# Where a routed expert layer hands over from its early tiles to its late ones: order of VectorE's steps, TensorE's filler products, SyncE's row numbers and GpSimd's scatters

## What is computed

```python
xn = layernorm(x)
# feed-forward part of layer 0 (after its own attention, which gives x_mid)
h2     = rmsnorm(x_mid, ln2_w)                       # (2048, 128)
top1   = argmax(h2 @ Wr + br)                        # one of E = 8 experts for each token
u      = h2 @ W1[top1] + b1[top1]                    # 512 columns
y      = (u[:256] * sigmoid(u[256:])) @ W2[top1] + b2[top1]
x      = x + attention(xn) + x_mid + y
# layer 1: layernorm(x), a state-space block and a four-matrix gated network, added to x
```

## Time and profile before

| | |
|---|---|
| median of 3 runs | 592.8 us (592.77, 592.80, 595.66) |
| profiled execution, its own time | 592.8 us |
| its span, first to last instruction | 590.9 us |
| TensorE busy | 557.3 us, 94% |
| ScalarE busy | 471.3 us, 80% |
| VectorE busy | 396.6 us, 67% |
| GpSimd busy | 121.2 us, 21% |
| mean granted clock of TensorE | 0.997 |

### The profile page before, as it was taken

The page is one execution under the profiler, slowest core; times in us unless marked ns, Lnnn a source line. Parts: engine busy times, 40 slices in busy tenths (PEclk is TensorE's granted clock), DMA queues, the critical chain, the costliest instruction groups (busy, mean ns, idle before and its releaser), DMA issues.

```text
span 590.9 us, 11199 instructions
## 1 busy us (share of the span) xinstructions
PE 557.3 (94%) x3932; PEld 330.4 (56%) x3932; DVE 396.6 (67%) x1056; ACT 471.3 (80%) x670; POOL 121.2 (21%) x161
## 2 busy tenths in 40 slices
PE   6799999999999999999998899798799999999998
PEld 3344333443443434334435587386678887887887
DVE  6884877576354353486618565886798698698773
ACT  6599999999999999998987465479696785786673
POOL 2063312030110021010710277112010020020010
PEclk9999999999999999999999999999899999999999
DMA  6212002025222220030317231200000000000000
GB/s 218 49 29 72 2 10 64 2 82 161 91 109 91 108 91 2 17 128 0 108 45 236 57 94 49 80 2 0 0 2 2 1 18 1 2 18 1 2 19 18
DMA packets 30982, 30.72 MB, mean 52 GB/s; under 512 B 6848, under 2 KB 20960, under 8 KB 30928
## 3 DMA queue, kind: packets, MB, share of 16 engines
q1 hardware_dynamic: 29680, 27.45, 14.9%
q0 software_dynamic: 1248, 2.57, 1.2%
HBM read 13.44 MB, written 12.89 MB: 45 GB/s over the span
## 4 chain that ended last, share of the span: by engine, by line
PE 70%; DVE 14%; ACT 6%; issue 5%; DMA 3%; POOL 1%; SPq 1%; DVEq 0%; ACTq 0%; POOLq 0%
PE ps L1423 18%; PE ps L1402 9%; PE ps L92 6%; PE ps L94 6%; PE ps L93 6%; PE ps L1732 2%; ACT r L1005 2%; PE ps L1503 2%; PE ps L1605 1%; PE ps L1316 1%; PE ps L1771 1%; PE ps L1774 1%; PE ps L1495 1%; DMA row<-in_f_kn 1%; PE ps L1737 1%
## 5 line engine op out<-in xcount | busy, mean ns | idle before, releaser
L1005 ACT ACTIVATE r<-ps 128x1024 f32<-128x1024 f32 x272 | 257.4, 1039 | 16.6 <-PE ps L1402 14.6
L1423 PE MATMUL ps<-r 128*32 128x512 f32 (+3 forms) x1280 | 144.8, 539 | 0.9 <-DVE r L2192 0.5
L857 POOL TENSOR_SCALAR_AFFINE_SELECT r<-r 128x512 f32<-128x512 f32 (+1 forms) x80 | 47.1, 590 | 206.7 <-ACT r L1005 206.4
L1402 PE MATMUL ps<-r2r 32*128 32x512 f32 (+3 forms) x640 | 79.2, 445 | 2.1 <-ACT r L1005 1.3
L1402 PEld LDWEIGHTS ps<-r2r 32*128 32x128 f32 x640 | 35.4, 182 | 44.0 <-issue 19.4
L904 POOL TENSOR_TENSOR r<-r 128x512 f32<-128x512 f32 x16 | 22.1, 1383 | 149.9 <-ACT r L1216 130.5
L1423 PEld LDWEIGHTS ps<-r 128*32 128x32 f32 x1280 | 27.7, 108 | 40.5 <-issue 27.0
L94 PE MATMUL ps<-r2r 128*128 128x512 f32 (+1 forms) x104 | 39.0, 375 | 0.0
L93 PE MATMUL ps<-r2r 128*128 128x512 f32 (+1 forms) x88 | 33.4, 379 | 0.0
L1288 PE MATMUL ps<-consts 128*128 128x512 bf16 x86 | 22.6, 400 | 7.8 <-DMA consts<-in_consts 4.2
L873 POOL DMA_INDIRECT rows_by_token<-r x23 | 24.3, 1058 | 17.5 <-ACT r L1068 12.6
(11 more groups left out here) (438 smaller groups left out, 1191.7 us busy)
## 6 DMA issues: line engine op xcount, KB each, us to landing
rows_by_expert<-r SPq DMA_DIRECT2D x34, 258.0 KB, 2.6
r2r<-r2r SPq DMA_DIRECT2D x56, 64.0 KB, 2.0
r<-in_f_W SPq DMA_DIRECT2D x1, 2048.0 KB, 9.4
r<-rows_by_expert SPq DMA_DIRECT2D x23, 64.5 KB, 1.9
res<-in_x SPq DMA_DIRECT2D x4, 256.0 KB, 3.7
r<-in_g_h1T SPq DMA_DIRECT2D x1, 1024.0 KB
r<-in_g_h2T SPq DMA_DIRECT2D x1, 1024.0 KB
r<-rows_by_token SPq DMA_DIRECT2D x4, 256.0 KB, 3.9
```

The costliest lines, as they stand in the source:

```text
L857: pool.affine_select(blk, blk, pattern, ALU.is_ge, nothing, base=0, channel_multiplier=-1).then_inc(s_msk, 1)
L1005: act.activation(probs[:, n % PBUFS, :, :], ps[:, b:b + 2, :], ACT.Exp).then_inc(s_exp, 1)
L1402: m = pe.matmul(ps[:, 2 * (n % SBUFS) + h, at:at + TB - query], kst[32 * j:32 * j + 32, group, P * kt:P * kt + P], qst[32 * j:32 * j + 32, ...
L1423: m = pe.matmul(ps[32 * j:32 * j + 32, 6, query:TB], vp[:, kt, group, :], probs[:, (2 * v + j // 2) % PBUFS, j % 2, at:at + TB - query], s ...
```

## The change

Five places are edited.

1. VectorE: `activated(1)` moves from ahead of `late_placed` to behind `rows_scaled` of tiles 14 and 15. The expert numbers (`expert_i`) and flag columns (`pick`) of tiles 5 to 22 are made ahead of the row numbers, not behind them, and the first of them is no longer waited for by itself.
2. TensorE: behind `first_down(4)` come four times a wait for a count from GpSimd and two filler products, then three more, the wait for all scatters, and eight. Before there were the wait and seven.
3. TensorE, in the loop: the wait for the high half of the group's rows stands in front of the bias product, not behind it.
4. SyncE: four row numbers are read ahead of the wait for the scatters, not two.
5. GpSimd: a count (`s_pace`) behind each of the last four row scatters; and the results are scattered in the order of their tiles, 0 to 22.

```diff
--- before.py
+++ after.py
@@ -427,6 +427,7 @@
         s_slot = sem("slots_ready")
         s_exp_t = sem("tile_experts_ready")
         s_scat = sem("rows_scattered")
+        s_pace = sem("rows_moved_by_gpsimd")
         s_hs = [sem(f"slot_rows_loaded{g}") for g in range(NG)]
         s_rows = sem("tile_rows_ready")
         s_hse = sem("first_slot_rows_loaded")
@@ -791,10 +792,10 @@
                 sp.dma_start(dst, io[name].broadcast_to([P, n])).then_inc(s_l1w, 16)
 
             sp.wait_ge(s_rows, 2)
-            ahead = [first_row(t) for t in range(AHEAD, AHEAD + GROUP)]
+            ahead = [first_row(t) for t in range(AHEAD, AHEAD + 2 * GROUP)]
             sp.wait_ge(s_scat, 16 * NT)
             for t in range(AHEAD, SLOTS):
-                r = ahead[t - AHEAD] if t < AHEAD + GROUP else first_row(t)
+                r = ahead[t - AHEAD] if t < AHEAD + 2 * GROUP else first_row(t)
                 sp.dma_start(hs_[:, t, :], hbuf[bass.ds(r, P), :]).then_inc(s_hs[(t - AHEAD) // GROUP], 16)
 
             sp.wait_ge(s_ysc, 16 * SLOTS)
@@ -867,17 +868,13 @@
             for i in range(NT - TPB, NT):
                 pool.wait_ge(s_h2, 2 if i < NT - 2 else 3)
                 rows_scattered(i)
-
-            def tokens_scattered(t):
+                pool.sem_inc(s_pace, 1)
+
+            for t in range(SLOTS):
                 pool.wait_ge(s_tok, 1 if t < AHEAD else (t - AHEAD) // GROUP + 2)
+                pool.wait_ge(s_yev, t + 1)
                 pool.indirect_dma_start(tbuf, bass.IndirectOffsetOnAxis(ap=token_u[:, t:t + 1], axis=0),
                                         ysb[:, t, :], None).then_inc(s_ysc, 16)
-
-            for t in range(AHEAD, SLOTS):
-                pool.wait_ge(s_yev, t + 1)
-                tokens_scattered(t)
-                if t % 2 == 0 and t - AHEAD < 2 * AHEAD:
-                    tokens_scattered((t - AHEAD) // 2)
 
             pool.memset(hst, 0.0).then_inc(s_ch, 1)
             pool.memset(xc[:, :, 0, 0:HALO], 0.0).then_inc(s_halo, 1)
@@ -1570,8 +1567,12 @@
             first_down(3)
             first_activations_transposed(4)
             first_down(4)
+            for i in range(TPB):
+                pe.wait_ge(s_pace, i + 1)
+                kept_busy(1, 2)
+            kept_busy(1, 3)
             pe.wait_ge(s_scat, 16 * NT)
-            kept_busy(1, 7)
+            kept_busy(1, 8)
             slots_transposed(0)
             pe.wait_ge(s_exp_t, 2)
             pe.wait_ge(s_wsp, len(W1LOW))
@@ -1582,10 +1583,10 @@
                     cols_ = bass.ds(e * (2 * HID), 2 * HID)
                     dst = ps[:, 2 + t % 2, :]
                     x = slice(P * t, P * t + P)
+                    pe.wait_ge(s_xsh, (t - AHEAD) // GROUP + 1)
                     pe.wait_ge(s_moea, t - 1)
                     pe.matmul(dst, pick[0:STACK, t:t + 1].broadcast_to([STACK, P]), biases[:, 0:2 * HID],
                               start=True, stop=False)
-                    pe.wait_ge(s_xsh, (t - AHEAD) // GROUP + 1)
                     pe.matmul(dst, xsh[:, x], w1h[:, cols_], start=False, stop=False)
                     pe.matmul(dst, xsh[:, x], w1l[:, cols_], start=False, stop=False)
                     pe.wait_ge(s_xsl, (t - AHEAD) // GROUP + 1)
@@ -2404,10 +2405,10 @@
             late_expert()
             rows_scaled(range(NT - TPB, NT - 2))
             dve.sem_inc(s_h2, 1)
-            activated(1)
             late_placed()
             rows_scaled(range(NT - 2, NT))
             dve.sem_inc(s_h2, 1)
+            activated(1)
             dve.wait_ge(s_cnts, 2)
             total = ps[:, SHARED, 0:E]
             over_ei = over_k.rearrange("p (e i) -> p e i", e=E)
@@ -2426,12 +2427,12 @@
             dve.wait_ge(s_slot, 2)
             step.alone(dve.tensor_tensor(tiles_passed[:, at], passed[:, at, 0:E - 1], along(step_up[:, 0:E - 1], n),
                                          ALU.mult))
+            step.mark(dve.tensor_copy(expert_i[:, at], expert[:, at]))
             step.alone(dve.tensor_reduce(lead_t[:, at], tiles_passed[:, at], X_AXIS, ALU.add))
+            dve.tensor_scalar(pick[:, at], expert[:, at], modulo, None, ALU.is_equal).then_inc(s_exp_t, 1)
             step.alone(dve.scalar_tensor_tensor(rows_f[:, at], tile_no[:, 0:n], early_used[:, 0:1], lead_t[:, at],
                                                 ALU.add, ALU.subtract))
             rows_of_tiles(at)
-            step.alone(dve.tensor_copy(expert_i[:, at], expert[:, at]))
-            dve.tensor_scalar(pick[:, at], expert[:, at], modulo, None, ALU.is_equal).then_inc(s_exp_t, 1)
             dve.wait_ge(s_hse, 16 * AHEAD)
             tokens_of_slots(range(AHEAD))
             activated(4)
```

## The result

The changed kernel took 597.71 us (median, 595.75 to 600.48), the kernel before 593.46 us (591.86 to 596.04) beside it: ratio 1.0068, 95% interval 1.0052 to 1.0084, some 4 us. Forecast were +3.0 us and a range that ended at 597.0. Of the 1.9 us between 595.8 and 597.71, 0.66 is the kernel before, which took 593.46 us here and not 592.8; the change itself came out at +4.25 us.

A forecast was written before the change was run, and what follows sets the result against it. TensorE was taken as the bound, busy throughout the loop over tiles 5 to 22, so a later loop start delays the end. Terms: +3.24 - 0.2 = +3.0 us on 592.8, giving 595.8 us; range 593.8 to 597.0.

The forecast's parts named there:

- fillers start later: TensorE's fillers behind tile 4's down product: start at 332.39 us, not 331.01, through tile 1's late activation.
- twelve more fillers, less the old 0.62 of idle: TensorE ahead of the slot rows' transposes: 19 fillers in line, not 7, take 4.15 us; alone +1.86.
- group 1 early: Start of TensorE's loop: four row numbers read ahead bring tile group 1's rows early, -0.2 us.
- T0: Start of TensorE's transposes of the slot rows, ahead of the loop: from 333.30 to 336.54 us, +3.24.
- Rival A: TensorE's first expert tiles: not late, slack hides the late activation, only fillers cost; 594.5 us, chance 0.13.
- rival B: TensorE ahead of the loop: new fillers run while it waits for the scatters, not slower; 592.6 us, chance 0.07.
- Tile 1's activation goes behind the last scaled rows: VectorE ahead of TensorE's first tiles: activation ends 1.62 us later, tile 1's transposes come 1.55 late.
- Rival D: Lower-clock stretch from 416.13 us: falls elsewhere, 594.1 us (0.09), or another such stretch comes, 597.5 (0.05); chance 0.14.
- Bias product behind the high rows' wait: TensorE's loop: bias product starts after ScalarE's copy; 0 to 0.25 us, taken as 0; later groups find the wait passed.
- At T0 the fillers buy no speed: TensorE around T0: clock was already 1.00 around the gap there, so more fillers gain no speed.
- Rival C: SyncE's row loads: each row number costs 1.09 us, so loads take the fillers' place; 596.3 us, chance 0.12.
- The ports: VectorE beside GpSimd's moved scatters: shared-port rule could block up to 0.97 us each; trace disagrees, sum unchanged.

The follow-up runs named there:

- e14: Changed kernel with six filler products in TensorE's gap ahead of tile 1's transposes, against the kernel before: 1.0073, 596.13 us.
- e1: Kernel before with only the 19 fillers and GpSimd's four counts put in: 1.0026 against the kernel before.
- e13: Changed kernel with nothing edited, compared a second time with the kernel before: 1.0102, 598.11 us.
- e15: Changed kernel with six fillers in the gap and the loop's wait back behind the bias product, against the kernel before: 1.0051, 595.05 us.
- e10: Kernel before with only the loop's wait for the high half moved ahead of the bias product, second try: 1.0008 against the kernel before.
- e9: Kernel before with only GpSimd's token scatters put in tile order, 0 to 22: 0.9999 against the kernel before.
- e2: Kernel before with only tile 1's activation moved behind the scaled rows of tiles 14 and 15: 1.0020 against the kernel before.
- e16: e11's kernel with eleven fillers in place of seven: 1.0009 against the kernel before.
- e3: Changed kernel with tile 1's activation put back ahead of the late slots: 1.0033 against the kernel before.
- e4: Changed kernel with six fillers in the gap ahead of tile 1's transposes, activation still late: 1.0050 against the kernel before.
- e11: Kernel before with four row numbers, expert numbers and flags ahead of row numbers, and token order, second try: 1.0012 against the kernel before.
- e7: Changed kernel with one wait and seven fillers as before the change: 0.9944 against the kernel before, on a chip with stalls.
- e5: Kernel before with only the loop's wait for the high rows moved ahead of the bias product: 1.0009 against the kernel before, on a chip with stalls.
- e8: Kernel before with three row numbers read ahead and eight fillers in the gap at 414 us: 0.9984 against the kernel before, on a chip with stalls.
- e12: Kernel before with the token order and eight fillers in TensorE's gap at 414 us: 0.9981 against the kernel before, 591.44 us.
- e6: Kernel before with four row numbers, flags ahead of row numbers and the token order: 0.9977 against the kernel before, on a chip with stalls.

## Why the forecast was too low

| term of the sum | forecast | measured | from |
|---|---|---|---|
| fillers start later | +1.38 | +1.43 | e14, 8.26 - 6.83 |
| twelve more fillers, less the old 0.62 of idle | +1.86 | +1.81 | e1, 10.93 - 9.12 |
| clock behind the gap | 0 | +1.64 when it falls | e13, 14.00 - 12.36 |
| GpSimd's counts, row numbers, flags first | 0 | 0 | +4.09; hidden in e14 |
| group 1 early | -0.2 | -0.22, but by the later T0 | e15, 35.63 - 35.85; e1 has -0.25 with two row numbers |
| wait ahead of the bias product | 0 (0 to 0.25) | +0.7 | e10 0.72; e14 less e15, 0.73 |
| token order | 0 | 0 | e9 |

Of e13's profile these make the whole: T0 +4.88, loop +0.42, behind it +0.12, and slot numbers 0.42 earlier by chance, together the 5.0 between 595.9 and 590.9.

*The delay and the fillers.* T0 without the fall is +12.36, 3.24 later than before, the very figure of the forecast; that it is the same to the last digit is luck, since two terms missed by 0.05 in opposite directions. Tile 1's transposes came 1.57 late and the fillers 1.43, so 0.14 of the wait ahead of tile 4's transposes came back, near the 0.17. Rival A (first tiles not late) falls by e2, rival B by e1, where all nineteen stand in one line. The 0.2 for group 1 had the right size and the wrong reason: e1 and e2, which read two row numbers ahead as before, have loops of 35.60 and 35.68, and e16, with four and T0 bound by the landing, has 35.79. A later T0 finds the rows of group 1 there in any case.

*The step that failed: "Tile 1's activation goes behind the last scaled rows", priced as 1.55 us of delay.* A delay of a TensorE product is also a gap in TensorE's work, and the products behind it were priced by their durations at 2.4 GHz. They ran at 1.2 GHz instead. The numbers were all there: its last product ends at about 323.5, the next would start at 325.18, and the earlier trace rows show what followed 2.12 us of idle elsewhere. Rival D had the mechanism, but took it as a stretch that might come by chance, at 0.05; that its time (597.5) is close to the 597.71 measured is in part luck, since the wait priced below and the 0.66 of the kernel before are in the 597.71 too. e2 shows that the edit makes it, e3 and e4 that it goes with the gap, in two ways: activation back, or the gap filled. It seems not to come in each execution: over 45 executions of the changed kernel the mean clock is 0.9919 (34 at 0.991 or below with a median of 598.34 us, 11 above with 596.26), against 0.9952 for e4 (3 of 12 at 0.991 or below) and 0.9947 for the kernel before in the session of e1 to e4 (9 of 35). A mean doesn't tell where the clock fell, so this is a count of falls anywhere. The Trainium skill, "TensorE: Matmul & The Clock Gate", Why this matters for your kernels, speaks for a tensor queue without idle gaps; the prediction weighed it at T0, where the kernel before had clock 1.00, and not at the gap that the change opens. e13 against e14 goes the way of that advice, at a gap shorter than those for which the page gives it.

*The second step that failed: "Bias product behind the high rows' wait", taken as 0.* In the first step the reasoning held: in e14 the first high product starts 1.04 behind T0 (338.42, from 337.38), in e15 also 1.04 (336.99, from 335.95), though the bias product itself is 0.73 later. What I had not priced is that "later groups find the wait passed" is not free: about 0.06 us at each of the later groups, 0.7 in all with the start of the loop. Why a passed wait in this place (behind the reading of the expert's number into a register) is felt and behind the bias product is not, no row shows.

*"At T0 the fillers buy no speed".* True for the kernel before, with 0.62 us of idle. With the later loads of e11 the idle is 1.22 and the clock fell in its profile, with a loop 1.27 longer than e16's; four more fillers (e16) closed that gap at no cost to T0. Eleven would do there; e7 shows that nineteen hold T0 back by some 1.9 us beyond the landing of the loads. Rival C is off: four numbers took 2.6 us in e11 (+4.48 to +7.05), or 0.64 each, where I had 0.55, and it stayed hidden behind the fillers.

*The ports.* The prediction gives the rule of the Trainium skill, "SBUF — State Buffer", SBUF: two separate sides, too widely. That section limits it to VectorE instructions in a two-port mode or with two inputs in SBUF. The activation has one input in SBUF and one in PSUM, so its 0.42 us beside GpSimd's issue agrees with the page.

Open: the difference between the two comparisons (1.0068 and 1.0102), of which the clock explains some by how often it falls, and the stalls of e5 to e8.

## What to carry to other kernels

When an edit makes TensorE wait somewhere, price two things: the delay, and the products behind the wait at the lower clock, if the trace shows falls behind other gaps; a 1.4 us gap cost 1.4 us once and then 1.6 more. Filler products belong into such a gap, as many as fit, and not in line in front of work that is ready: six in the gap won 1.64 us of T0, twelve in line cost 1.81. And in a loop bound by its own queue, count a wait moved in front of the first product of a step as a cost, even if it has long passed.

## What was not expected of the hardware

- The granted clock fell behind idle times of TensorE of 1.22 us (e11), 1.42 (e2, e13) and 2.12 us; behind 0.62 ahead of T0 it stayed at 1.00. Such a stretch at the lower level was 3 to 4 us long, with the engine busy in nearly all of it, and cost 1.3 to 1.64 us (e11, e12, e13).
- The length of the gap alone doesn't decide. Behind the wait for the first block of tokens the clock stayed at 1.00 in the kernel before (1.55 us idle) and in e1, e2 and e3 (1.62, 1.65 and 1.69), and fell in e16 and e15 (1.96 and 2.03); behind the same 2.12 us it fell in 12 profiles and stayed in 4. What else it hangs on is open.
- A wait that has long passed cost about 0.06 us ahead of a bias product (e10).
- On one chip the same kernel took 604 us, not 593, and four row numbers read by SyncE with the wait for the scatters took 5.8 us (e6, +4.47 to +10.24), not 2.6; in e7, on the same chip, they took 2.7 (+6.81 to +9.51).
